# A second tile of lookahead in attention, and the residual loads and output stores moved from SP's queue to GpSimd's

## What is computed

```python
mask = pos[None, :] < pos[:, None]
scores = jnp.einsum('bhtd,bsd->bhts', q, k) * scale
scores = jnp.where(mask[None, None, :, :], scores, NEG_BIG)
attn = jax.nn.softmax(scores, axis=-1)
out = jnp.einsum('bhts,bsd->bhtd', attn, v)
...
x = _layernorm(x + _L0_attn_ref(...))
hidden = jax.nn.silu(x @ W1.T) * (x @ W3.T)
hidden = fwht(hidden)
x = _layernorm(x + hidden @ W2.T)
```

## Time and profile before

| what | us |
|---|---|
| two timed runs | 3146.69 and 3324.54, median 3235.62 |
| the profiled execution, whole | 3121.13 |
| its span, first to last instruction, slowest core | 3119.3 |
| spans of the eight cores | 3105.4 to 3119.3 |
| PE busy in the span | 2521.4 (81%) |
| ACT, DVE, POOL busy | 673.5, 552.5, 149.4 |

### The profile page before, as it was taken

How to read it: one execution, slowest core, us unless ns; L and a number is a source line. 1 busy time by engine, 2 the same in 40 slices (tenths; PEclk the granted TensorE clock), 3 DMA queues, 4 the chain that set the end, 5 groups by cost and what they waited for, 6 DMA issues and landing times.

```text
span 3119.3 us, 28280 instructions; the slowest of 8 cores (3105.4 to 3119.3 us)
## 1 busy us (share of the span) xinstructions
PE 2521.4 (81%) x10080; PEld 952.5 (31%) x10080; DVE 552.5 (18%) x760; ACT 673.5 (22%) x1227; POOL 149.4 (5%) x280
## 2 busy tenths in 40 slices
PE   3667755677788999888289999999999989786894
PEld 1222211111122222233134444444444434332342
DVE  1111124444333332312200000000000000001002
ACT  1211112233345555500611111111111110001001
POOL 1110000000000000000000000000000000000000
PEclk8768865566789999999599999999999999897997
DMA  7654353222100000021222222222222225445554
GB/s 217 195 155 135 108 175 86 82 75 81 54 14 1 1 1 1 1 81 41 95 81 68 73 69 68 68 68 73 69 68 68 68 69 152 144 143 159 143 153 146
DMA packets 96461, 276.70 MB, mean 89 GB/s; under 512 B 11716, under 2 KB 11844, under 8 KB 91976
## 3 DMA queue, kind: packets, MB, share of 16 engines
q0 software_dynamic: 34512, 139.48, 14.6%
q1 hardware_dynamic: 61816, 135.43, 13.6%
HBM read 224.54 MB, written 50.33 MB: 88 GB/s over the span
## 4 chain that ended last, share of the span: by engine, by line
PE 77%; ACT 7%; DVE 7%; issue 4%; DMA 4%; ACTq 0%; DVEq 0%; POOL 0%; SPq 0%; POOLq 0%
PE pb L177 72%; PE pb L179 4%; ACT GA L239 2%; DVE GA L243 2%; DMA GA<-X1S 1%; ACT GA L425 1%; DVE pb L422 1%; ACT GA L655 1%; DMA GA<-XBT 1%; DMA W2P<-GA 1%; DVE GA L462 1%; DVE LNS L734 1%; ACT GA L568 1%; ACT GA L549 1%; ACT GA L556 0%
## 5 line engine op out<-in xcount | busy, mean ns | idle before, releaser
L177 PE MATMUL pb<-GA 128*128 128x512 bf16 x8576 | 2125.9, 392 | 256.0 <-ACT GA L425 79.2
L177 PEld LDWEIGHTS pb<-GA 128*128 128x128 bf16 x8576 | 833.5, 99 | 1478.8 <-issue 653.3
L425 ACT ACTIVATE GA<-pb 128x512 bf16<-128x512 f32 x576 | 340.9, 597 | 442.3 <-PE pb L177 303.1
L179 PE MATMUL pb<-GA,CB 64*64 64x512 bf16 x512 | 140.6, 534 | 214.1 <-ACT GA L239 117.8
L177 PE MATMUL pb<-GA,CB 128*1 128x512 bf16 (+1 forms) x704 | 274.2, 404 | 2.8 <-DVE GA L635 2.8
L655 ACT ACTIVATE GA<-pb 128x512 bf16<-128x512 f32 x128 | 69.6, 594 | 840.7 <-PE pb L177 840.7
L635 DVE TENSOR_TENSOR GA<-GA,pb 128x512 bf16<-128x512 f32 x128 | 82.3, 683 | 914.5 <-ACT GA L632 883.8
L243 DVE CAST GA<-pb 128x512 bf16<-128x512 f32 x128 | 88.5, 691 | 450.2 <-PE pb L179 450.2
L422 DVE TENSOR_TENSOR pb<-pb,GA 128x512 f32<-128x512 f32 x128 | 88.6, 698 | 332.9 <-PE pb L177 332.4
L179 PEld LDWEIGHTS pb<-GA,CB 64*64 64x64 bf16 x512 | 37.1, 116 | 313.0 <-issue 312.8
L177 PEld LDWEIGHTS pb<-GA,CB 128*1 128x1 bf16 (+1 forms) x704 | 58.1, 83 | 200.9 <-issue 186.0
(11 more groups left out here) (45 smaller groups left out, 391.4 us busy)
## 6 DMA issues: line engine op xcount, KB each, us to landing
GA<-W2P SPq DMA_DIRECT2D x256, 256.0 KB, 2.7
GA<-W2T POOLq DMA_DIRECT2D x128, 256.0 KB, 4.6
W2P<-GA SPq DMA_DIRECT2D x128, 256.0 KB, 5.0
GA<-W1S POOLq DMA_DIRECT2D x64, 512.0 KB, 3.8
GA<-W3S POOLq DMA_DIRECT2D x64, 512.0 KB, 4.0
GA<-XBT POOLq DMA_DIRECT2D x8, 2048.0 KB, 12.0
GA<-WQS POOLq DMA_DIRECT2D x4, 2048.0 KB, 9.7
GA<-XOWN SPq DMA_DIRECT2D x1, 8192.0 KB, 37.7
```

The costliest lines, as they stand in the source:

```text
L177: return e.matmul(out, lhsT, rhs, start=start, stop=stop, skip_group_check=True)
L179: return e.matmul(out, lhsT, rhs, start=start, stop=stop, skip_group_check=True, tile_position=tp)
L425: texp = em.op("s", lambda e, qp=qp, slot=slot: e.activation(pbuf[slot], qp[:], AF.Exp, scale=SC), waits=_mx(dep, pbuf_rd[slot]))
```

## The change

`pend` becomes a list of up to two tiles: AV and RS of tile i are emitted behind QK of tile i+2 and no longer behind QK of tile i+1; at a group's end both are emitted. The X1S loads and the OUT stores go from SP's list to POOL's. Since the X1S loads no longer stand behind W2P loads that waited for `p5w0`, both buffers get that wait themselves.

```diff
-                pend = None
+                pend = []
...
-                        if pend is not None:
-                            rs_mm = emit_avrs(*pend)
-                        pend = (slot, sig, it == 0, it == niter - 1, texp)
+                        if len(pend) == 2:
+                            rs_mm = emit_avrs(*pend.pop(0))
+                        pend.append((slot, sig, it == 0, it == niter - 1, texp))
                         it += 1
-                rs_mm = emit_avrs(*pend)
+                while pend:
+                    rs_mm = emit_avrs(*pend.pop(0))
...
-        x1rl_rd = [None, None]
+        x1rl_rd = [p5w0, p5w0]
...
-                    tx = em.op("y", lambda e, k=k, dh=dh, sl=sl: e.dma_start(
+                    tx = em.op("g", lambda e, k=k, dh=dh, sl=sl: e.dma_start(
...
-                to = em.op("y", lambda e, k=k, osl=osl: e.dma_start(OUT[k], outst[osl]),
+                to = em.op("g", lambda e, k=k, osl=osl: e.dma_start(OUT[k], outst[osl]),
```

## The result

The changed kernel takes 0.9805 of the time of the kernel before (95% interval 0.9761 to 0.9849): 1.95% faster, or 61 us of 3121. The interval lies on both sides of 2%, so that it is faster is measured, and that it is faster by over 2% is not. The medians of all runs are 3084.9 us (11 runs) and 3150.2 us (10 runs); in some executions of either kernel one half of the chip runs at a lower clock, and the ratio leaves these out. The profiled execution took 3064.7 us with a span of 3063.1, 56.2 us less than before. The prediction had 3030, and 101 us for the sum. The measured time lies in its range and the sign is right; 45 of the 101 us aren't there.

What follows compares the result with a forecast made beforehand. It took PE's waits for the exp to bound attention, and PE plus a chain at quarter ends the last stage. Gains of 74 and 27 us from 3121 gave 3020, set at 3030 for run offset; range 2995 to 3110.

Steps and rivals of the forecast that it cites:

- the case that was forecast: Whole kernel: both parts work, 3030 us, own range 2995 to 3060, chance 0.78.
- rival C: Attention: AV follows QK no sooner than 0.31 us, clock stays low longer in blocks 0 to 3; 3063 us, chance 0.09.
- signs of being wrong: Turns of 0.92 with the exp early; clock under 0.9 in blocks 4 to 7; load chain above 5.5 us a turn.
- Blocks 4 to 7, 41 us: Late attention blocks: lookahead of two shortens 416 turns and 16 group ends, gaining 40.8 us.
- 0.84n + 3.11: Attention, blocks 4 to 7: time in us of a group of n tiles after the change, against 0.92n + 3.58 before.
- rival E: Attention, blocks 4 to 7: idle of about 1.7 us behind QK2 lowers the clock; slower, 3153 us if half the turns fell; 0.03.
- Blocks 0 to 3, 33 us: Early attention blocks: gains at group starts and on masked tiles, together 33 us.
- lookahead gains nothing in such a turn: Attention, blocks 0 to 3: a low-clock turn is 1.48 us of pure matmul, so lookahead gains nothing there.
- Last stage, 26.6 us: Last stage, queue change: 27 at the second end plus 2, less 1.4 and 1, makes 26.6 us.
- I take 0.3 us for each of the three late loads: Quarter ends of the last stage: each late X1S load costs 0.3 us more from POOL, 0.9 an end.
- the W2T row's end of the range: Last stage: if all loads cost as W2T, POOL's farthest row at 4.6 us, the gain is 16 us.
- the layer norm that stood there runs beside the matmuls: Second quarter end, last stage: layer norm overlaps matmuls, as DVE and ACT have nothing else for some 110 us.

Runs made afterwards that it cites:

- f4: Kernel before (lookahead of one) with a group's closing work behind the sixth QK of the next group, blocks 2 to 7: group of 32 tiles 32.5 us.
- e3: Changed kernel with a group's closing work behind the sixth QK of the next group instead of the third, blocks 2 to 7: profiled span 3008.1 us.
- e4: Kernel before with a group's closing work behind the first QK of the next group instead of the third: clock 0.92, group of 32 tiles 35.5 to 36.4 us.
- g1: Changed kernel with a group's closing work behind the fourth QK of the next group, blocks 2 to 7: clock 1.00, group of 32 tiles 29.37 us.
- f2: Changed kernel with only the X1S loads back on SP's queue: 0.9808 of the kernel before, last stage 550.8 us.
- f3: Changed kernel storing only 256 of 2048 output columns of blocks 0 to 3: third quarter 112.0 us.
- f1: e3 with residual loads in mid-quarter into the add's buffer, output stores on POOL for two quarters, then SP: 0.941 of the kernel before.

## Why the prediction was right or wrong

**The sign and the range: right, in part by luck.** Unmasked turns fell to 0.84 us, three score banks suffice, the exp's waits fell, at the second end PE idles 16.1 us behind DVE as foreseen, and f4 confirms that a turn of 0.92 is the exp's doing, since it stays when the sums are no longer waited for. But 3064.7 lies outside the case that was forecast (2995 to 3060) and in the range only because this was drawn to 3110. It is within 2 us of rival C's 3063, and that is luck: neither of C's conditions holds, as QK with AV takes 0.53 us in every dense turn and the clock of blocks 0 to 3 rose. Three errors, +12, -28.5 and -23 us, made the number. That the gain is over 2%, given 0.88, is not shown; and C's own 58 us lie under those 2%, so its chance doesn't belong there. Of the signs of being wrong one came (a load turn of 6.0 us, over 5.5), and a clock of 0.90 in blocks 4 to 7 stands on the line of another.

**Blocks 4 to 7, 41 us: the mechanism was right, its price left out the clock.** The step that failed is "that is 0.84n + 3.11", which took the pause behind QK2 at its own length. The pause was foreseen, and so was the fall of the clock behind it, but only as rival E with a chance of 0.03, argued away by a PE that is 90% busy at 0.96. That was the busy share of a kernel without the pause. The pause costs two to four turns at 1.48 instead of 0.84 us, and a group of 32 is 1.9 and 2.9 us over its formula by turns, the 16 groups 37.9. The timeline has 49 row sums at the low level in them (16 in the kernel before), and 49 x 0.64 = 31 us of the 37.9; the other 7 weren't traced. E's decision, that 158 low turns would lose all, wasn't reached. e3, e4 and g1 show the pause as the cause from three sides.

**Blocks 0 to 3, 33 us: undersized.** Between the second reciprocal and block 4 the gain is 42.9, where the same sum gives 31. On the median core it is 37.2, so half of the excess is that the kernel before was slow on its slowest core. The excess is mostly in blocks 1 and 2: on the slowest cores, in block 1 a group takes 22.1 to 22.4 us and took 25.0 to 26.9, 4 us and not 2.7. The step "lookahead gains nothing in such a turn" held the number of low turns as it was, and it fell: from 84 to 62 of 96 in block 1 and from 69 to 58 of 112 in block 2, 14 and 7 us at 0.64 each. Why the clock rises earlier wasn't tried.

**Last stage, 26.6 us: one term right, two mis-sized.** The second end was to gain 27 in all and gained 22.2. The term "I take 0.3 us for each of the three late loads" was wrong: 0.9 to 1.0 a turn in the last end, 0.5 of it landing (4.0 us for 3.6) and the rest a later issue. Over the twelve loads the turns cost 10.8 us more; that is the W2T row's end of the range. At that end the prediction's own terms leave 18 us (26.6 less 12 x 0.7) and not the 16 that it names; the measured 3.9, or 8.6 on the median core, lies under both. The W1S row was of loads issued long before need. Behind the last turn the tail takes 29.1 us instead of 25.9, 2.6 more than the 0.5 allowed for the last store. Not all of it is the store: in f2, which has its stores on POOL too, that tail takes 27.4. And "the layer norm that stood there runs beside the matmuls" counted DVE, ACT and POOL, but not the 4 MB of stores beside the W2P loads, which cost 9 us in the third quarter (f3; 7 on the median core). This overlap, put at nothing, is the step that failed here.
The rule of the Trainium skill on first-byte latency ("DMA: Bandwidth & Descriptors", section "Latency and other measured facts") gave an estimate of 4.8 us for the twelve loads: nearer than the 3.6 of my sum, still under half of the measured 10.8. Its rule that a second issuing engine saves only the time to issue (section "Issuing engines are not separate DMA queues") doesn't hold for the second end, where 22 us went because SP no longer waits for ACT ahead of ready loads; the rest of that section, that the transfers interleave on the same DMA engines, is what the third quarter paid for.

## What to carry to other kernels

Deeper lookahead moves work behind whatever PE waits for at a loop's end; look there for a new pause before counting the gain, and move the wait too, since each alone gave 12 and 20 us here and both together 67 (9, 16 and 63 on the median core). Price a pause of PE by its own length and by the turns at the low clock that follow it. For DMA queues, ask which transfer stands behind a wait that isn't its own: here moving the stores gave 17 us (f2 against the kernel before), moving the loads that sit on the critical chain took 13.5 of them back, and loading them earlier gave 66 (f1 against e3). And read a stage on all cores before its gain is called 4 us: the slowest core of one run and of another differ by as much.

## What was not expected of the hardware

Two waits of 0.70 and 0.93 us with one matmul between them are followed by two to four turns at the low clock, 3 to 6 us of otherwise dense work; 0.51 and 0.16 with four matmuls between never were, in the 15 groups behind the first of blocks 4 to 7. From the changed kernel's 0.90 to g1's 1.00 it took moving the closing work by one tile. Under the pause the loss alternates from group to group, about 1 us more in every second one. Four 1 MB stores issued from POOL beside 256 KB loads from SP stretch single loads from 2.8 us (their median) to over 9, though the DMA engines were at 0.58 of their time in that quarter.
